# A recurrent two-layer kernel: GpSimd's order round two scan states, TensorE's order behind the transposes, two steps moved on VectorE

## The chip, the cores and the metric

One core of one Trainium2 chip. The metric is the device time of one execution in microseconds. The core's engines are TensorE (PE, with its weight loads as PEld), VectorE (DVE), ScalarE (ACT), GpSimd (POOL) and SyncE (SP), which here only issues DMAs. Each engine works through its own instructions strictly in the order in which the program issues them; between engines there are only semaphores.

## The reference, cut to what matters

```python
x = L0_attn_x                                  # (4, 1024, 128)
xn = _layernorm(x)
s = retention(xn)        # q, k, v, scores times a decay mask, summed over the past
g = silu(ternary_ffn(xn))# h = silu(x w1) * (x w2); gelu(h h1); gelu(h h2); w3
x = x + s * g            # layer zero
xn = _layernorm(x)
# layer one, left side (a state-space scan)
x_ssm, gate = split(xn @ W_in + b_in)
x_conv = silu(causal_conv4(x_ssm) + conv_b)
B, C = split(x_conv @ W_x + b_x)               # 16 states each
h = exp(-exp(A_log)) * h + x_conv[:, :, None] * B[:, None, :]   # over time
y = sum_n(C * h) + D * x_conv
s = (y * silu(gate)) @ W_out + b_out
# layer one, right side: the top half of the tokens by a router score go through an FFN
g = silu(xn + [token is in the top half] * sigmoid(score) * ffn(xn))
x = x + s * g
```

## The kernel before, in words

**Tiling.** The four sequences of 1024 tokens are cut into eight units of 512 tokens (`HALF`). A unit's features lie on the 128 partitions, its tokens along the free axis. The scan over time has 128 x 16 = 2048 rows, so each unit has 16 scan steps k = 0 to 15, one tile of 128 rows by 512 tokens each.

**Stages.** The program runs through periods p = -1 to 8 (`PERIODS`), each of 16 slots s (`slots`, those of p = -1 from slot 9). In period p the units have roles (`units`): n = p does layer one's front (its norm, convolution, gate, B, C, score), v = p + 1 does layer zero, w = p + 2 gets its layer-zero norm, t = p - 1 finishes its scan, ranking and token update, e = p - 2 is put out. Slots 0 to 7 hold the scan steps 8 to 15 of t, slots 8 to 15 the steps 0 to 7 of n (`scanned`). A function `slot(p, s)` in each engine's block lists what that engine does in a slot: the order is written out by hand, and an engine whose next instruction waits holds up all that stands behind it.

**One scan step.** SP spreads 8 rows of `xc` over 128 partitions by DMA (`spread_x` into `xs`, a ring of 5); DVE multiplies with B (`times_b` into `xbank`; `Bt` for k < 3, `bbank` after) and scans (`scan` into `hs`, a ring of 8); POOL multiplies with C (`weigh_states`); PE sums four steps at a time into `ybank` (`gather_y`, quads 0 to 3). `gate_y` (DVE) multiplies `ybank` by the gate into `yg`, which PE projects (`project_out`) for DVE's `output` and POOL's `add_output`.

**Hidden layers of layer zero.** Each 128x512 tile is made on PE (`hidden`), taken twice on ACT (`plain`, and rounded, `hidAh`/`hidBh`), and POOL subtracts the two (`low_hidden` into `hidAl`/`hidBl`); PE's next layer needs the difference of all four tiles. `plain` is a ring of three, so ACT's tile i waits for POOL's tile i - 3. z, h1 and h2 have four tiles each: h1 is made in slots 5 to 8, h2 in slots 10 to 13.

**Norms.** DVE takes the statistics (`stats_l0`, slot 7; `stats_l1`, slot 2), POOL makes the root (`rstd_l0`, slot 8, before that slot's scan state; `rstd_l1`, slot 2), ACT normalizes (`norm_l0`, slot 9, before `take_u`, which empties the bank that the first h2 tile needs; `norm_l1`, slot 2), PE transposes (`retention_in`, slot 9, before h2; `norm_to_features`, slot 3).

**Banks.** `bank0d` holds in turn z2(1), scores, z2(3), outer and s of layer zero: each waits until DVE has taken the one before (`L0_DVE`). `bank1a` holds xnT, conv, gate, B, C, score and its column in that order (`L1_ACT`), each after ACT has taken the one before.

**PE before, slots 3 to 9:** z1(3), z2(3), mod_down, norm_to_features | outer, gather_y quad 2, convolve | project_out, gate, h1(0) | B, h1(1), C | rank, h1(2), score | h1(3), score_column, quad 3 | rank, retention_out, retention_in.

## Time and profile before

| | |
|---|---|
| median of 3 runs | 537.83 us (537.45 to 539.37) |
| the profiled execution | 537.29 us, of which the span is 535.5 us |
| PE busy | 441.1 us, 82% of the span |
| DVE busy | 394.2 us, 74% |
| POOL busy | 387.8 us, 72% |
| ACT busy | 291.4 us, 54% |
| the chain that ended last | PE 34%, DVE 22%, issue 17%, POOL 16%, ACT 8%, DMA 2% |

All times of the trace are microseconds from the start of the span. The stretch from slot 14 of one period to slot 14 of the next shows in the trace as the distance between two quad-0 sums in `ybank`; six such distances, from 114.5 to 455, are the steady part, ahead of them is the filling, behind them (80 us) the last unit, in which layer zero has nothing left to do. The page's letters are the engines; "idle before" is what an engine waited ahead of an instruction, and the name behind the arrow is what ended the wait. No engine is busy all of the time, and the chain changes engine many times in a period; the rows below are from the period of n = 3 (its slots 0 to 15 lie between about 231 and 289) unless they say otherwise.

### The profile page before, as it was taken

The page shows a single profiled execution, that of the slowest core. Times are in us where ns is not written, and L with a number is a line of the kernel's source. Part 1 is how long each engine was busy: PE and PEld are TensorE (multiplying, and loading weights), DVE is VectorE, ACT ScalarE, POOL GpSimd, SP SyncE. Part 2 cuts the span into 40 slices and gives each one's busy share as a digit, 9 for nine tenths or more (in the row PEclk, how much of TensorE's full clock was granted, in tenths as well). Part 3 has the DMA queues.
Part 4 walks back from the last instruction along what each step waited for, and adds up shares of the span by engine and source line. Part 5 has one row for each costly group of instructions (what it writes and reads, how often), then busy time and mean ns, then how long its engine had stood idle before and what let it go on. Part 6 is the DMA issues. An engine that isn't in the chain of part 4 may idle for free.

```text
span 535.5 us, 6095 instructions
## 1 busy us (share of the span) xinstructions
PE 441.1 (82%) x1796; PEld 261.6 (49%) x1807; DVE 394.2 (74%) x683; ACT 291.4 (54%) x475; POOL 387.8 (72%) x317
## 2 busy tenths in 40 slices
PE   0794968898989898998889897989799889875843
PEld 0573645654555555654565455545555457321221
DVE  2282042959779895879688986798698949978985
ACT  3763654685467646763667556764676466333300
POOL 1672561788499859987699859984998679863682
PEclk9996979899999999999999999999999999898865
DMA  8300004421342215320633144312523053306330
GB/s 319 140 21 4 1 1 125 112 78 40 88 110 79 80 35 161 99 80 20 194 84 78 40 138 127 76 54 62 144 73 96 20 159 79 98 23 174 86 91 20
DMA packets 25379, 46.97 MB, mean 88 GB/s; under 512 B 3072, under 2 KB 4096, under 8 KB 25088
## 3 DMA queue, kind: packets, MB, share of 16 engines
q1 hardware_dynamic: 24336, 45.13, 29.9%
q10 hardware_dynamic: 1008, 1.41, 0.8%
q8 instruction: 18, 0.29, 0.2%
q14 instruction: 17, 0.14, 0.1%
HBM read 42.33 MB, written 4.19 MB: 87 GB/s over the span
## 4 chain that ended last, share of the span: by engine, by line
PE 34%; DVE 22%; issue 17%; POOL 16%; ACT 8%; DMA 2%; SPq 0%; DVEq 0%; POOLq 0%; ACTq 0%
PE bank0a L940 18%; DVE hs L1371 9%; DVE xbank L1348 6%; POOL hs L556 6%; PE bank0a L1059 5%; POOL hidAl L518 2%; ACT xn L692 2%; POOL hidBl L518 2%; PE ybank L1085 2%; PE bank1a L1020 2%; POOL g L530 2%; POOL xr L538 1%; POOL q L507 1%; DMA Bt<-w_in 1%; DVE st L1276 1%
## 5 line engine op out<-in xcount | busy, mean ns | idle before, releaser
L556 POOL TENSOR_TENSOR hs<-hs,Ct 128x512 f32<-128x512 f32 x127 | 170.9, 1350 | 34.5 <-DVE hs L1371 22.3
L518 POOL TENSOR_TENSOR hidAl<-plain,hidAh 128x512 fp32r<-128x512 f32 x48 | 63.7, 1327 | 39.3 <-ACT hidAh L651 33.2
L1371 DVE TENSOR_TENSOR_SCAN hs<-decay,carry,xbank 128x512 f32<-128x512 f32 x63 | 80.5, 1278 | 8.0 <-DVE xbank L1348 0.5
L518 POOL TENSOR_TENSOR hidBl<-plain,hidBh 128x512 fp32r<-128x512 f32 x48 | 67.0, 1396 | 26.4 <-ACT hidBh L651 18.5
L1371 DVE TENSOR_TENSOR_SCAN hs<-decay,xbank 128x512 f32<-128x512 f32 x64 | 78.0, 1219 | 5.6 <-DVE xbank L1348 0.5
L1348 DVE TENSOR_TENSOR xbank<-xs,bbank 128x512 f32<-128x512 f32 x104 | 71.5, 687 | 1.3
L650 ACT ACTIVATE plain<-bank0a,col 128x512 f32<-128x512 f32 x64 | 44.1, 689 | 44.7 <-PE bank0a L940 43.5
L940 PE MATMUL bank0a<-hidBh,hTh 128*128 128x512 f32 x128 | 57.8, 452 | 1.7 <-ACT q L683 1.7
L940 PE MATMUL bank0a<-hidAh,hTh 128*128 128x512 f32 x128 | 56.4, 441 | 1.7 <-ACT q L683 1.7
L940 PE MATMUL bank0a<-hidAl,hTh 128*128 128x512 f32 x128 | 51.7, 404 | 0.0
L940 PE MATMUL bank0a<-hidBl,hTh 128*128 128x512 f32 x128 | 50.7, 396 | 0.0
L1085 PE MATMUL ybank<-hs,gat 128*32 128x512 f32 x254 | 36.9, 648 | 16.2 <-POOL hs L556 16.1
L1348 DVE TENSOR_TENSOR xbank<-xs,Bt 128x512 f32<-128x512 f32 x24 | 26.7, 1114 | 27.6 <-ACT Bt L638 19.6
L1020 PE MATMUL bank1a<-ynT,w_conv 128*128 128x512 f32 (+3 forms) x64 | 34.3, 645 | 0.0
L1319 DVE SCALAR_TENSOR_TENSOR beats<-srow,scol,earlier 128x512 bf16<-128x512 f32 x32 | 34.3, 1071 | 0.0
L758 ACT ACTIVATE fh<-bank0a,col 128x512 f32<-128x512 f32 x32 | 21.3, 686 | 23.7 <-PE bank0a L1059 23.6
L1059 PE MATMUL bank0a<-ynT,lw 128*128 128x512 f32 x64 | 33.8, 635 | 0.0
L1271 DVE TENSOR_TENSOR sc<-bank0d,sc 128x512 f32<-128x512 f32 x8 | 5.5, 691 | 36.0 <-ACT sc L670 36.0
L940 PEld LDWEIGHTS bank0a<-hidBh,hTh 128*128 128x128 f32 x128 | 24.3, 190 | 11.4 <-issue 3.1
L940 PEld LDWEIGHTS bank0a<-hidAh,hTh 128*128 128x128 f32 x128 | 24.7, 193 | 10.2 <-ACT q L683 2.5
L1068 PE MATMUL bank1d<-fh,w2l 128*128 128x512 f32 x56 | 29.3, 608 | 0.0
L638 ACT ACTIVATE xc<-bank1a,b_conv 128x512 f32<-128x512 f32 x8 | 5.5, 687 | 43.1 <-PE bank1a L1020 43.1
(190 smaller groups left out, 938.8 us busy)
## 6 DMA issues: line engine op xcount, KB each, us to landing
xs<-x_rows SPq DMA_DIRECT2D x128, 256.0 KB, 3.5
xt<-x_tok SPq DMA_DIRECT2D x8, 256.0 KB, 4.8
xr<-x_feat SPq DMA_DIRECT2D x8, 256.0 KB, 7.6
x_rows<-xc SPq DMA_DIRECT2D x8, 256.0 KB, 2.3
out<-xr SPq DMA_DIRECT2D x7, 256.0 KB, 2.3
fh<-h_w SPq DMA_DIRECT2D x1, 1024.0 KB, 9.6
hs<-h_w SPq DMA_DIRECT2D x1, 1024.0 KB, 11.4
lw<-l_w ACTq DMA_DIRECT2D x1, 640.0 KB, 5.3
```

The source lines that it names most:

```text
L518: pool.tensor_tensor(low[:, m, :], plain[:, k % NPLAIN, :], high[:, m, :].bitcast(F32), ALU.subtract).then_inc(hidden_low, 1)
L556: pool.tensor_tensor(h, h, Ct[:, hs_(u)], ALU.mult).then_inc(p_ready, 1)
L650: act.activation(plain[:, k % NPLAIN, :], bank[:], ACT.Gelu, scale=scale(kind + "_s", m))
L758: act.activation(fh[:, m, :], bank[:], ACT.Gelu_apprx_tanh, bias=scale("b1", m)).then_inc(l0_act_done, 1)
L940: last = pe.matmul(bank[:], w, x, start=(start and n == 0), stop=(stop and n == len(passes) - 1))
L1020: last = pe.matmul(bank1a[:, s:HALF], w_conv[:, k, :], ynT[:, t % NYNT, 0:HALF - s], start=(s == 0), stop=(k == 0))
L1059: pe.matmul(bank[:], W_1[:, ck(m)], ynT[:, t % NYNT, :], start=True, stop=True).then_inc(l0_act_full, 1)
L1068: last = pe.matmul((bank0d if t == UNITS - 1 else bank1d)[:], w2l[:, kt, :], fh[:, kt, :], start=(kt == 0), stop=(kt == KT - 1))
L1085: pe.matmul(ybank[rows, :], gat[:, at:at + P // QUAD], hs[:, step(u, QUAD * quad + j) % NSTATES, :], start=False, stop=(quad == NGRP // QU ...
L1319: dve.scalar_tensor_tensor(bt, row, s_i, earlier[:, at:at + HALF], ALU.subtract, ALU.is_lt).then_inc(beats_ready, 1)
L1348: dve.tensor_tensor(xbank[:], xs[:, i % NROWS, :], b, ALU.mult).then_inc(xb_ready, 1)
L1371: dve.tensor_tensor_scan(hs[:, i % NSTATES, :], decay[:, gr:gr + 1].broadcast_to([P, HALF]), xbank[:], 0.0 if u % 2 == 0 else carry[:, k:k ...
```

## The change

**GpSimd.** Before, slots 6 to 9 each began with one `low_hidden("h1")`, then (slot 8) `rstd_l0`, then the scan state. Now slots 6 and 7 begin with the scan states k = 14 and 15; behind 15 follow `rstd_l0(w)` and h1(0); h1(1) and h1(2) come ahead of the states k = 0 and 1 (slots 8 and 9), h1(3) behind the state k = 1. `weigh_update` goes from slot 6 to slot 10. **TensorE.** Behind the transposes of slot 3 comes the convolution, then project_out and B, and only then outer, quad 2 and the gate; **ScalarE** takes B before the gate. **VectorE.** `stats_l1` stands behind z_product(1) in slot 1 instead of behind `times_b` of slot 2; `mask_scores` before z_product(2) instead of behind it; `memory` in slot 6 instead of 4; `gate_y` in slot 11 instead of 9. In the prologue POOL does one h1 tile fewer before `rstd_l0(1)`.

```diff
-        L1_ACT += [(_k, _n) for _k in ("xnT", "conv", "gate", "B", "C", "score", "score_col")]
+        L1_ACT += [(_k, _n) for _k in ("xnT", "conv", "B", "gate", "C", "score", "score_col")]
...
                 if v is not None:
                     if 1 <= s < 1 + KT:
                         low_hidden("z", v, s - 1)
-                    elif 6 <= s < 6 + KT:
-                        low_hidden("h1", v, s - 6)
+                    elif s in (8, 9):
+                        low_hidden("h1", v, s - 7)
...
-                if w is not None and s == 8:
-                    rstd_l0(w)
                 if u is not None:
                     weigh_states(u, k)
+                if w is not None and s == 7:
+                    rstd_l0(w)
+                if v is not None and s in (7, 9):
+                    low_hidden("h1", v, 0 if s == 7 else 3)
...
-                if t is not None and s == (1 if t == UNITS - 1 else 6):
+                if t is not None and s == (1 if t == UNITS - 1 else 10):
                     weigh_update(t)
...
-            for m in range(KT - 1):
+            for m in range(KT - 2):
                 low_hidden("h1", 0, m)
...
                     if s == 5:
                         convolved(n)
+                        take_B(n)
                         take_gate(n)
...
-                    if s == 6:
-                        take_B(n)
-                    elif s == 7:
+                    if s == 7:
                         take_C(n)
...
-                        elif s == 4:
-                            outer(v)
...
-                    if s in (1, 4) and t is not None:
-                        gather_y(t, 1 if s == 1 else 2)
+                    if n is not None and s == 4:
+                        convolve(n, (3, 2, 1, 0))
                     if s == 5 and e is not None and e != UNITS - 2:
                         project_out(e)
-                    if n is not None:
-                        if s == 4:
-                            convolve(n, (3, 2, 1, 0))
-                        elif s == 5:
-                            project("gate", n, W_IN[:, P:2 * P])
-                        elif s == 6:
-                            project_x("B", n, W_B)
+                    if n is not None and s == 5:
+                        project_x("B", n, W_B)
+                    if v is not None and s == 5:
+                        outer(v)
+                    if s in (1, 5) and t is not None:
+                        gather_y(t, 1 if s == 1 else 2)
+                    if n is not None and s == 5:
+                        project("gate", n, W_IN[:, P:2 * P])
...
-                    elif s == 2:
-                        stats_l1(n)
...
+                if v is not None and s == 2:
+                    mask_scores(v)
                 if v is not None and s < KT:
                     z_product(v, s)
+                if n is not None and s == 1:
+                    stats_l1(n)
                 if v is not None:
-                    if s == 2:
-                        mask_scores(v)
-                    elif s == 4:
+                    if s == 6:
                         memory(v)
...
-                    elif t < UNITS - 1 and s == 9:
+                    elif t < UNITS - 1 and s == 11:
                         gate_y(t)
```

## Rows read from the trace of the kernel before

**Rows 1.** Stretches by period: length; busy time of PE, PEld, DVE, ACT, POOL; clock; DMA.

```profile
114.50:171.10 56.60, 50.99 (x223) 30.49 (x225) 44.38 (x83) 34.23 (x58) 44.38 (x37) 1.00 0.30 79
228.00:285.90 57.90, 51.85 (x224) 30.88 (x230) 47.21 (x88) 35.05 (x59) 47.43 (x39) 1.00 0.34 92
...
400.60:455.00 54.40, 50.52 (x221) 30.47 (x226) 43.95 (x66) 31.81 (x52) 45.07 (x35) 1.00 0.33 88
455.00:535.00 80.00, 51.23 (x165) 18.92 (x166) 65.66 (x98) 20.28 (x31) 47.95 (x39) 0.79 0.31 82
```

**Rows 2.** Timeline of POOL, n = 3: start, duration, line, tiles, idle before.

```profile
259.85 1.27 POOL L518 TENSOR_TENSOR hidBl<-plain,hidBh 128x512 fp32r<-128x512 f32 x1 [5.15 <-ACT hidBh L651]
...
266.98 1.27 POOL L556 TENSOR_TENSOR hs<-hs,Ct 128x512 f32<-128x512 f32 x1
...
269.43 1.02 POOL L485 TENSOR_TENSOR rstd<-ve,half_neg 128x4 f32<-128x4 f32 x1
```

**Rows 3.** Timeline of PE, n = 3: z2(3), outer, project_out, C, quad 3, h2(0).

```profile
244.09 0.48 PE L940 MATMUL bank0d<-xnTh,w12h 128*128 128x512 f32 x1 [1.79 <-DVE sc L1240]
...
246.88 1.13 PE L913 MATMUL bank0d<-xn,xt 128*128 128x128 f32 x8 [0.79 <-DVE plain L1264]
...
253.13 1.02 PE L1108 MATMUL bank1d<-Bt,lw 128*128 128x512 f32 x2
...
260.40 1.12 PE L1030 MATMUL bank1a<-xc,lw 128*128 128x512 f32 x2 [0.55 <-ACT Bt L638]
...
268.30 1.06 PE L1085 MATMUL ybank<-hs,gat 128*32 128x512 f32 x8 [1.31 <-POOL hs L556]
...
273.83 0.50 PE L940 MATMUL bank0a<-hidBh,hTh 128*128 128x512 f32 x1 [0.58 <-ACT q L683]
```

**Rows 4.** Timeline of ACT, n = 3: ynT, xc, Bt, bbank (keep_B), norm_l0.

```profile
246.13 0.60 ACT L638 ACTIVATE ynT<-bank1a 128x512 f32<-128x512 f32 x1 [0.68 <-PE bank1a L999]
...
253.39 0.69 ACT L638 ACTIVATE xc<-bank1a,b_conv 128x512 f32<-128x512 f32 x1 [5.42 <-PE bank1a L1020]
...
259.66 0.69 ACT L638 ACTIVATE Bt<-bank1a,col 128x512 f32<-128x512 f32 x1
...
267.85 0.61 ACT L748 ACTIVATE bbank<-Bt 128x512 f32<-128x512 f32 x1
270.89 1.65 ACT L692 ACTIVATE xn<-xt,ve,rstd 128x128 f32<-128x128 f32 x4 [2.42 <-POOL ve L488]
```

**Rows 5.** Timeline of DVE, n = 3: stats_l1, scan, mask, times_b(0), gate_y, token_weights.

```profile
239.76 0.86 DVE L1276 BATCH_NORM_STATS2 st<-yn 128x6 f32<-128x128 f32 x4
...
241.28 1.21 DVE L1371 TENSOR_TENSOR_SCAN hs<-decay,xbank 128x512 f32<-128x512 f32 x1
...
243.26 0.68 DVE L1240 TENSOR_TENSOR sc<-bank0d,mask 128x512 f32<-128x512 f32 x1
...
260.92 0.76 DVE L1348 TENSOR_TENSOR xbank<-xs,Bt 128x512 f32<-128x512 f32 x1 [2.40 <-ACT Bt L638]
...
269.51 0.69 DVE L1380 TENSOR_TENSOR Bt<-ybank,gate 128x512 f32<-128x512 f32 x1 [3.46 <-PE ybank L1085]
...
279.54 0.67 DVE L1334 SCALAR_TENSOR_TENSOR g<-bank1d,g 128x512 f32<-128x512 f32 x1
```

**Rows 6.** Instructions of line 556: duration min/median/max.

```profile
L556 POOL TENSOR_TENSOR hs<-hs,Ct x127: 1262/1278/1815, 98.4 to 525.0; 128x512 f32<-128x512 f32 x127
```

**Rows 7.** Timeline of PE in period 0: retention_in.

```profile
100.30 0.65 PE L892 MATMUL bank0a<-ident,xn 128*128 128x128 f32 x4 [1.30 <-ACT xn L692]
```

**Rows 8.** Timeline of PE in period 6: quad 3.

```profile
439.84 1.06 PE L1085 MATMUL ybank<-hs,gat 128*32 128x512 f32 x8 [1.26 <-POOL hs L556]
```

**Rows 9.** Timeline of ACT in period 7: ynT.

```profile
470.83 0.60 ACT L638 ACTIVATE ynT<-bank1a 128x512 f32<-128x512 f32 x1 [0.81 <-PE bank1a L999]
```

**Rows 10.** Timeline of PE in period 7: quad 2.

```profile
471.88 1.06 PE L1085 MATMUL ybank<-hs,gat 128*32 128x512 f32 x8 [1.08 <-POOL hs L556]
```

**Rows 11.** Timeline of DVE in period 7: times_b(0).

```profile
483.66 0.70 DVE L1348 TENSOR_TENSOR xbank<-xs,Bt 128x512 f32<-128x512 f32 x1 [2.66 <-DMA xs<-x_rows]
```

## The prediction

> **What bounds the kernel now.** I read the page's busy shares first, then the table of stretches, the list of waits, the chain, and last the timelines of one period, engine by engine. The stretches show that PE is busy 50.99 us of 56.60 in the first steady one and 51.85 of 57.90 in that of n = 3, at full clock, while DVE and POOL have some 10 us of slack each [rows 1]. So a steady period is PE's own work plus about 6 us in which PE waits, and five such stretches and a sixth without w make up the time from 114.5 to 455 (rows 1 show the first, the third and the sixth) [rows 1]. The reader is to see in PE's timeline where these 6 us lie: 1.79 before z2(3), 0.79 before outer, 0.55 before C, 1.31 before quad 3, 0.58 before h2(0) [rows 3], which makes 5.0; the rest lies before the transposes ahead of it. Each has another engine behind it. z2(3) waits for the mask on DVE, whose stream is gapless there [rows 5]. C waits for ACT, which has to empty `bank1a` of B and does that only behind h1(0), at 259.66 [rows 4]. Quad 3 waits for POOL's state 15 at 266.98, and that is the important one: POOL sits idle 5.15 us until 259.85 for the first h1 tile, with state 14, add_output, weigh_update, state 15 and the root of the norm all queued behind it [rows 2]. The root (269.43) is what ACT's norm_l0 waits for 2.42 us [rows 2, 4], and h2(0) on PE follows norm_l0 through the transposes and take_u, 273.83 - 270.89 = 2.94 us after its start [rows 3, 4].
>
> **The change in one steady period, from PE's start of slot 0.** (a) Mask first takes its 0.68 us from z2(3)'s wait [rows 5]. Against that, `stats_l1` starts earlier by about 0.6 us, but times_b of slot 2, which ran ahead of it, now stands behind it: it was 0.69 long and the scan behind it came directly at 241.28 [rows 5]. Net the scan is 0.2 to 0.3 later. z2(3) starts 0.4 earlier. The statistics' earlier end is worth at most 0.1, since POOL is busy with a z tile until it takes the root, 0.1 behind DVE. Running sum -0.4.
> (b) The transposes come 0.4 earlier. The 0.79 us before outer goes, but the convolution now stands directly behind ynT, which ACT takes 0.60 us long right behind the transposes [rows 4]: a wait of 0.7 to 0.8 in its place. Net 0.
> (c) Convolution, then project_out, 1.02 us [rows 3], which covers ACT's xc, 0.69 us and some 0.2 of handover [rows 4]; B then finds xc ready. Its matmuls (as large as project_out's) only move from behind h1(0) to ahead of it. Outer (1.13 as its first matmul group stands in the row [rows 3]) and quad 2 only move too, and they give ACT the time to empty B before the gate. Quad 2's states are finished long before; the ring of eight `hs` tiles needs it for the states 0 to 3 of n, 5 us later still. `memory` in slot 6 finds outer done, and retention_out wants it only in slot 9; load_tok, on SP in slot 6 behind the spreads, waits for outer in slot 5 and delays nothing. At the end of h1(1) the sum is still -0.4.
> (d) C no longer waits for ACT: 0.7 us counted from h1(1)'s last start to 260.40 (0.55 as listed [rows 3]). Sum -1.1, at the end of h1(3).
> (e) POOL. Its 5.15 us idle stretch [rows 2] takes in state 14, add_output, state 15 and the root; DVE has scan 15 by about 257 and the statistics of w by 258.8, so the root is done by about 260.2, and h1(0) goes at 260.2 instead of 259.85, a delay of 0.4 that ACT doesn't feel: it wants that place in `plain` only for h1(3), 5 us on. So quad 3 finds state 15 seven microseconds old: -1.3, sum -2.5.
> (f) norm_l0 no longer waits for POOL. It now stands behind keep_B, which ran from 267.85 for 0.61 [rows 4] and moves by (d): 267.85 + 0.61 - 1.1 = 267.35 instead of 270.89 [rows 4], -3.5. PE gets to the transposes at about 269.0, as ACT is done with them. h2(0) follows 2.94 later: 270.3 instead of 273.83. **Sum -3.5**; in even n, where the mask comes in a slightly tighter stream, I get -3.3. I take 3.35.
> (g) Can the rest follow? DVE: times_b(0) loses its 2.40 and gate_y its 3.46 us of waiting [rows 5]; with Bt taken at about 253 and the spread rows landed by 257 the first is limited by DVE alone. DVE comes to token_weights at about 275 instead of 279.54 [rows 5], in odd n ahead of PE's shift; in even n it waits there for PE's ranks and moves with it, as before. gate_y in slot 11 is done at 271.5, PE's quad 0 wants it at 282. weigh_update in slot 10 is done at about 271, token_weights wants it at 275. POOL's h1(3) ends at about 268, h2 wants it at 271.8. From low_xn on POOL has the same order as before, shifted with PE, and its last h2 tile had 1.5 us in hand before w3. So the whole 3.35 stays.
>
> **The other periods.** p = 1 to 5: 5 x 3.35 = 16.8. p = 0 has no scan states before slot 8, so POOL is not late; what is left is C's 0.7 and part of the 1.30 us before the transposes [rows 7], less B's xc, which no project_out covers: 1.0. p = 6 has no w: (a) to (e) with quad 3's 1.26 [rows 8], 2.4. p = 7 has neither v nor w and is set by DVE and a DMA: ynT is taken by 471.43 [rows 9], the convolution started only behind quad 2, which waited 1.08 for state 11 and began at 471.88 [rows 10]. Now it starts with ynT, and the statistics come 0.5 sooner: 1.9 us earlier, and xc, its store, the spread and times_b(0), which waited 2.66 us for that DMA [rows 11], follow; from there to the end DVE has hardly a gap and the same work. In the prologue POOL does rstd_l0(1) one tile sooner but waits there for DVE either way; the held-back tile has 5 us before h2. Nothing.
> Sum: 16.8 + 1.0 + 2.4 + 1.9 = 22.1. The profiled execution took 537.29 us, of which 535.5 span; it is 0.54 under the median of 537.83. 537.3 - 22.1 = 515.2, against the median 515.7. I say **515.4**.
>
> **What the sum doesn't show.** The extra price of two engines working side by side where POOL was idle. A POOL multiplication takes 1.26 us alone and 1.82 at worst beside DVE, median 1.28 [rows 6]. Four instructions move into the gap: between 0 and 2.2 us, of which 5 us of slack to quad 3 swallow all. Hence 0, with the worst case among the rivals.
> The Trainium skill speaks against filling that gap: its page "SBUF — State Buffer", section "Who interferes with whom", has VectorE's two-SBUF-input tensor_tensor and GpSimd's reads share a port pair that one holds and the other waits for. By it every moved state could cost itself up to one DVE instruction; the trace agrees that the same POOL form has two lengths, and the sum by that rule would be that of the rival R1 at most.
>
> **Rivals.**
> R1, POOL becomes the bound behind the gap. From h1(3) on ACT (266.7) to the last h2 tile, POOL has 12 instructions, now with weigh_update's place right ahead of h2. At 1.28 they take 15.4 us, at 1.75 21, so they end between 282 and 287.7; PE's w3 wants the last at 286.7. At worst 1.0 us of the gain is lost in each of five periods, and if low h1(3) comes late too, 1 more: 515.4 + 5 to 10 = 520 to 525. For: POOL is 47.43 us busy of 57.90 [rows 1], and of the new 54.4 that is 87%. Against: its median is 1.28 [rows 6].
> R2, more than I count: the waits I left (0.7 ahead of the convolution, 1.3 before z2(3), 0.6 before h2) shrink, or the last stretch gains from keep_B and the gate coming sooner: up to 1 us in six periods, 509. Against: each is one engine's latency.
> R3, nothing: the POOL wait was idle time that another chain (scan on DVE from slot 0 to 5, then PE) would have had anyway, and only C's and the mask's 1.1 us stay, given back in the next period's residual wait: 537. Against it speaks that quad 3 and h2(0) themselves stand waiting on PE [rows 3].
> R4, slower. POOL's head now waits for scan 15 and the statistics of w before it does any h1 tile. Were DVE late there, h1(3) on ACT would wait for a free `plain` and all of PE's h2 behind it. It decides from 4 us of DVE's delay against the replay, costs 1 us per us beyond that, and with 8 us late PE loses 4 - 3.35 net: 5 x 0.65 more than before, 540.5. For: DVE is gapless from slot 0 to 8. Against: it gets no new work, only 0.3 us from (a).
>
> **How the numbers follow.** Forecast (511 to 519.5) 0.66; R1 0.18; R2 0.08; R3 0.04; R4 0.04. The range for 8 in 10 takes in the forecast, most of R1 and a part of R2: 510 to 522.5. A measurement of this kernel can tell about 0.5% (2.7 us) from no change: faster 0.92, same 0.04, slower 0.04.
>
> **What would show it.** Steady stretches of 53.3 (even) to 54.4 (odd) us with PE busy unchanged; no POOL wait ahead of the states 14 and 15, and only a small one ahead of h1(0); no wait before C and quad 3; ACT's norm_l0 directly behind keep_B; a wait of 0.7 before the convolution; 1.3 before z2(3); times_b(0) and gate_y on DVE without waits; period 7's times_b(0) still waiting for its DMA. Wrong would be: h2 or w3 on PE waiting for POOL (R1), or ACT's h1(3) waiting for POOL (R4).

## The result and the profile after

The changed kernel takes **523.79 us** (median of 4 runs, 519.55 to 525.08) against 537.85 us (537.45 to 539.37) for the kernel before on the same chip: a ratio of 0.972, 95% interval 0.966 to 0.978. It is faster, as forecast, but by 14 us and not by 22, and the range (510.0 to 522.5) missed it by 1.3. Its profiled execution took 522.57 us, of which 520.8 span.

The same stretches of the changed kernel as [rows 1] (length; busy time of PE, PEld, DVE, ACT, POOL; granted clock; DMA share), cut at the same point of the period, with period 5 added as the third line:

```profile
115.40:170.05 54.65, 50.51 (x225) 30.49 (x228) 45.76 (x83) 34.20 (x58) 44.45 (x36) 1.00 0.31 78
224.00:278.70 54.70, 51.37 (x226) 30.87 (x227) 49.40 (x89) 34.99 (x59) 47.70 (x39) 1.00 0.36 100
332.60:388.70 56.10, 52.77 (x226) 31.49 (x227) 49.56 (x89) 34.86 (x59) 47.60 (x39) 0.97 0.31 88
388.70:441.30 52.60, 50.24 (x222) 30.56 (x226) 46.80 (x67) 31.99 (x52) 44.82 (x36) 1.00 0.32 92
441.30:520.00 78.70, 49.63 (x167) 18.76 (x166) 65.09 (x96) 20.14 (x31) 47.00 (x38) 0.83 0.28 83
```

PE has the same work in a shorter stretch: 3.3 us of waiting are left of 54.70 in the period of n = 3, where 6.05 were left of 57.90. DVE is busy 2.2 us longer there for the same tiles (49.40 against 47.21 in rows 1), POOL 0.3.

TensorE in the period of n = 3 (start, duration, line, tiles, idle before), to be laid beside [rows 3]; the lines are z2(3), the convolution, project_out, outer, quad 3 and h2(0):

```profile
240.17 0.47 PE L941 MATMUL bank0d<-xnTh,w12h 128*128 128x512 f32 x1 [1.91 <-DVE sc L1240]
242.95 1.10 PE L1021 MATMUL bank1a<-ynT,w_conv 128*128 128x512 f32 x2 [0.78 <-ACT ynT L640]
...
247.12 1.02 PE L1109 MATMUL bank1d<-Bt,lw 128*128 128x512 f32 x2
...
249.15 1.05 PE L914 MATMUL bank0d<-xn,xt 128*128 128x128 f32 x8
...
262.23 1.06 PE L1086 MATMUL ybank<-hs,gat 128*32 128x512 f32 x8
...
266.62 0.50 PE L941 MATMUL bank0a<-hidBh,hTh 128*128 128x512 f32 x1 [0.57 <-ACT q L685]
```

The waits before outer, C and quad 3 are gone; the convolution waits 0.78 for ynT; the wait before z2(3) has grown from 1.79 to 1.91 instead of falling to 1.3. POOL and ACT in the same stretch, beside [rows 2] and [rows 4]: POOL's states 14 and 15 with add_output's product between them, the root, h1(0) and h1(1); ACT's keep_B and norm_l0.

```profile
250.26 1.28 POOL L556 TENSOR_TENSOR hs<-hs,Ct 128x512 f32<-128x512 f32 x1
251.50 1.28 POOL L538 TENSOR_TENSOR xr<-g,xr 128x512 f32<-128x512 f32 x1
253.89 1.30 POOL L556 TENSOR_TENSOR hs<-hs,Ct 128x512 f32<-128x512 f32 x1 [1.12 <-DVE carry L1375]
255.29 1.46 POOL L485 TENSOR_TENSOR rstd<-ve,half_neg 128x4 f32<-128x4 f32 x1
256.83 0.20 POOL L488 TENSOR_TENSOR ve<-negmean,rstd 128x4 f32<-128x4 f32 x1
256.99 2.97 POOL L518 TENSOR_TENSOR hidBl<-plain,hidBh 128x512 fp32r<-128x512 f32 x2
```

```profile
263.17 0.61 ACT L750 ACTIVATE bbank<-Bt 128x512 f32<-128x512 f32 x1
263.69 1.64 ACT L694 ACTIVATE xn<-xt,ve,rstd 128x128 f32<-128x128 f32 x4
```

POOL's idle 5.15 us [rows 2] now hold both states and the root; ACT's norm_l0 stands directly behind keep_B. Quad 3's state is ready 7.0 us before PE wants it. This part of the forecast came true line by line.

The distances between the quad-0 sums (for n = 0 at 113.52 before and 114.39 after, then from one n to the next):

| | to n = 0 | p = 1 | 2 | 3 | 4 | 5 | 6 | 7 | from there to the end |
|---|---|---|---|---|---|---|---|---|---|
| before | 113.52 | 56.60 | 56.85 | 57.88 | 56.85 | 57.88 | 54.42 | 43.84 | 37.66 |
| changed | 114.39 | 54.65 | 53.89 | 54.71 | 53.89 | 56.14 | 52.61 | 41.59 | 38.93 |
| difference | +0.9 | -1.95 | -2.96 | -3.17 | -2.96 | -1.74 | -1.8 | -2.25 | +1.3 |
| forecast | -1.0 | -3.35 | -3.35 | -3.35 | -3.35 | -3.35 | -2.4 | -1.9 for both | |

The differences add up to -14.7 us where the forecast had -22.1. The seven us that are missing lie in four places: the filling (1.9), period 1 (1.4), period 5 (1.6), and the rest in small amounts in the other steady periods and in the end (2.5). Each row is one execution. In a second profile of the changed kernel (span 524.4 us) periods 1 to 6 have the same lengths to 0.15 us, but quad 0 of n = 0 starts at 115.71 and period 7 takes 43.30: what is said below of the filling and of period 7 holds for the profiled execution only. The experiments go after these places and after what each part of the change was worth.

### The profile page after: what moved, and what is told of

It is laid out like the page before. It is cut to its first block, busy times and chain, and to the rows that moved or that the text cites. A ratio compares the mean times of both kernels' runs of the same rounds, so it can differ in the third digit from the quotient of the medians.

```text
span 520.8 us, 6106 instructions
## 1 busy us (share of the span) xinstructions
PE 438.9 (84%) x1807; PEld 262.1 (50%) x1807; DVE 401.0 (77%) x683; ACT 291.4 (56%) x475; POOL 388.5 (75%) x317
## 4 chain that ended last, share of the span: by engine, by line
PE 59%; DVE 15%; ACT 10%; issue 9%; POOL 3%; DMA 3%; SPq 0%; DVEq 0%; ACTq 0%; POOLq 0%
PE bank0a L941 27%; PE bank1a L1021 6%; DVE hs L1371 5%; PE bank0a L1060 5%; DVE xbank L1348 4%; PE ybank L1086 3%; PE bank1a L1031 3%; PE bank1a L1006 3%; ACT xn L694 2%; DVE plain L1264 2%; DMA Bt<-w_in 2%; PE bank0d L914 1%; DVE st L1276 1%; PE ybank L1081 1%; PE bank0d L930 1%
## 5 line engine op out<-in xcount | busy, mean ns | idle before, releaser
L556 POOL TENSOR_TENSOR hs<-hs,Ct 128x512 f32<-128x512 f32 x127 | 164.2, 1295 | 44.0 <-DVE hs L1371 25.4
L518 POOL TENSOR_TENSOR hidAl<-plain,hidAh 128x512 fp32r<-128x512 f32 x48 | 67.3, 1407 | 16.9 <-ACT hidAh L653 10.7
L941 PE MATMUL bank0a<-hidBh,hTh 128*128 128x512 f32 x128 | 56.0, 438 | 1.7 <-ACT q L685 1.7
L941 PE MATMUL bank0a<-hidAh,hTh 128*128 128x512 f32 x128 | 55.3, 432 | 1.7 <-ACT q L685 1.7
L1086 PE MATMUL ybank<-hs,gat 128*32 128x512 f32 x254 | 35.8, 630 | 9.0 <-POOL hs L556 9.0
L1348 DVE TENSOR_TENSOR xbank<-xs,Bt 128x512 f32<-128x512 f32 x24 | 29.5, 1227 | 4.3 <-DMA xs<-x_rows 3.4
L941 PEld LDWEIGHTS bank0a<-hidAl,hTh 128*128 128x128 f32 x128 | 24.7, 193 | 6.8 <-issue 1.4
```

The costliest lines, as they stand in the source:

```text
L518: pool.tensor_tensor(low[:, m, :], plain[:, k % NPLAIN, :], high[:, m, :].bitcast(F32), ALU.subtract).then_inc(hidden_low, 1)
L556: pool.tensor_tensor(h, h, Ct[:, hs_(u)], ALU.mult).then_inc(p_ready, 1)
L941: last = pe.matmul(bank[:], w, x, start=(start and n == 0), stop=(stop and n == len(passes) - 1))
L1086: pe.matmul(ybank[rows, :], gat[:, at:at + P // QUAD], hs[:, step(u, QUAD * quad + j) % NSTATES, :], start=False, stop=(quad == NGRP // QU ...
L1348: dve.tensor_tensor(xbank[:], xs[:, i % NROWS, :], b, ALU.mult).then_inc(xb_ready, 1)
```

## Experiments

In the text all differences are taken between medians; the kernel before had medians of 537.76 to 538.69 beside these runs, so a difference of 1 us between two of them says little.

| | what is different | median us | range | ratio to before, 95% |
|---|---|---|---|---|
| changed | (measured again) | 523.79 | 520.13 to 526.16 | 0.970 (0.9675 to 0.9734) |
| 1 | changed, statistics back | 520.29 | 516.05 to 521.35 | 0.965 (0.9625 to 0.9672) |
| 2 | changed, statistics and mask back | 521.65 | 519.79 to 521.87 | 0.969 (0.9658 to 0.9711) |
| 3 | changed, two DVE instructions to ACT | 518.16 | 514.58 to 518.82 | 0.961 (0.959 to 0.9639) |
| 4 | changed, z1(3) repeated from period 0 | 514.63 | 513.81 to 516.41 | 0.955 (0.9521 to 0.9569) |
| 5 | changed, z1(3) repeated from period 1 | 519.02 | 517.97 to 520.61 | 0.964 (0.9605 to 0.966) |
| 6 | before, z1(3) repeated from period 0 | 535.27 | 532.77 to 536.62 | 0.995 (0.993 to 0.9965) |
| 7 | before with the new POOL order | 529.05 | 526.55 to 530.44 | 0.982 (0.9784 to 0.9864) |
| 8 | changed with the old POOL order | 548.27 | 547.36 to 551.35 | 1.020 (1.0154 to 1.0236) |
| 9 | before with the new DVE order | 549.48 | 546.5 to 550.01 | 1.020 (1.0168 to 1.0228) |
| 10 | as 8, B behind h1(0) | 542.69 | 536.82 to 544.9 | 1.007 (1.0032 to 1.0099) |
| 11 | 3 and a shorter 4 together | 511.51 | 508.57 to 515.21 | 0.950 (0.9459 to 0.9542) |

### The statistics of layer one (1)

```diff
+                    elif s == 2:
+                        stats_l1(n)
...
-                if n is not None and s == 1:
-                    stats_l1(n)
```

> Only stats_l1 goes back to slot 2, behind times_b; the mask stays first and all else is as changed. Theory port: in the changed kernel the short addition of eps in stats_l1 (line 1285) took 0.80 us instead of 0.21 because it now runs while GpSimd works on a z tile, so the early statistics gain nothing and the scan behind them, the mask and z2(3) come 0.8 us later than they could. Then line 1285 is back at about 0.2 us, z2(3) waits about 1.2 instead of 1.9 us, the steady periods are 0.6 to 0.8 us shorter (54.0 odd, 53.2 even), and the time is 4 us below the changed kernel's. Rival, what stands before z2(3) is no path: period and time as in the changed kernel (54.7 and 53.9, within 1 us).

The reason to try it is DVE's timeline of the changed kernel in slot 1: the last z product, the statistics (the second-last of them line 1285, an addition on 128x4 elements), times_b, scan, mask. Beside it stands POOL's z tile.

```profile
236.13 0.28 DVE L1281 BATCH_NORM_AGGREGATE mv<-st 128x2 f32<-128x6 f32 x3
236.45 0.80 DVE L1285 TENSOR_SCALAR ve<-mv 128x4 f32<-128x4 f32 x1
237.16 0.16 DVE L1286 TENSOR_SCALAR negmean<-mv 128x4 f32<-128x4 f32 x1
237.23 0.69 DVE L1348 TENSOR_TENSOR xbank<-xs,bbank 128x512 f32<-128x512 f32 x1
238.02 1.22 DVE L1371 TENSOR_TENSOR_SCAN hs<-decay,xbank 128x512 f32<-128x512 f32 x1
...
239.35 0.68 DVE L1240 TENSOR_TENSOR sc<-bank0d,mask 128x512 f32<-128x512 f32 x1
```

```profile
235.96 1.27 POOL L518 TENSOR_TENSOR hidAl<-plain,hidAh 128x512 fp32r<-128x512 f32 x1
```

Line 1285 ends at 237.25, POOL's tile at 237.23. The groups of that line, of the changed kernel and then of this one (count, busy us, mean ns, idle us before):

```profile
L1285 DVE TENSOR_SCALAR ve<-mv 128x4 f32<-128x4 f32 x8 | 5.8, 730 | 0.3
```

```profile
L1285 DVE TENSOR_SCALAR ve<-mv 128x4 f32<-128x4 f32 x8 | 2.3, 284 | 0.3
```

The means hide two lengths: in periods 1 to 6 the addition takes 209 to 221 ns in its old place and 802 to 817 in the new one; the two at the ends of the program take the same in both. So the early place put the addition beside a POOL tile, and it took 0.6 us longer; the tile of slot 1 stayed the thing that POOL had to finish before the root, so the statistics' earlier end bought nothing. With them back the steady periods are 53.1 and 53.9 instead of 53.9 and 54.7, z2(3) waits 1.1:

```profile
236.71 0.47 PE L941 MATMUL bank0d<-xnTh,w12h 128*128 128x512 f32 x1 [1.12 <-DVE sc L1240]
```

and the median is 3.5 us lower, near the theory's 4. The step of the statistics in the change costs 0.8 us a period, of which the longer addition is 0.6. The Trainium skill, "SBUF — State Buffer", section "Who interferes with whom", says that tensor_scalar can enter a mode in which it takes the port pair it has in common with GpSimd, and whoever holds that pair blocks the other for the whole instruction; the end of the 0.80 us together with POOL's agrees with that. That the instruction was in that mode no run here shows.

### Mask and statistics together (2)

```diff
-                if v is not None and s == 2:
-                    mask_scores(v)
                 if v is not None and s < KT:
                     z_product(v, s)
+                if v is not None and s == 2:
+                    mask_scores(v)
```

and the statistics back as in the run before.

> The changed kernel with both VectorE steps of slots 1 and 2 back where they were: the statistics of layer one behind times_b of slot 2, the mask behind z_product(2). Against the run with the statistics alone back (520.29, z2(3) waits 1.2 in its steady periods) this tells what the mask is worth. Theory, VectorE's part is worth nothing taken together, because the mask's gain is eaten by the statistics' port: 523 to 525 like the changed kernel, z2(3) waiting 1.6 to 1.9, and 0.4 to 0.5 more per period than with the statistics alone back. Rival, the mask's place is worth nothing and all of the statistics' loss is saved: 520 to 521, z2(3) waiting 1.2.

The steady periods are 54.6 and 53.7, against 53.9 and 53.1 with the mask first and 54.7 and 53.9 in the changed kernel; z2(3) waits 1.80 in the period of n = 3. So the mask's place is worth 0.65 us a period, the statistics' costs 0.8, together a little less than nothing. By the medians the kernel lies between, at 521.65: 1.4 above the run with the statistics alone back, and 2.1 below the changed kernel, which shows one fall of the clock more in its profile (below). Both expectations missed the time, 523 to 525 and 520 to 521. The wait of 1.80 is the theory's (1.6 to 1.9), and the mask is worth more than its 0.4 to 0.5 a period.

### The same statistics with two instructions on ACT (3)

```diff
             def norm_l1(t):
+                act.activation(ve1[:, cc], mv1[:, cc, 1], ACT.Copy, bias=EPS).then_inc(eps1, 1)
+                act.activation(negmean1[:, cc], mv1[:, cc, 0], ACT.Copy, scale=-1.0).then_inc(negmean1_ready, 1)
```

and lines 1285 and 1286 taken from DVE; the statistics stay in slot 1.

> stats_l1 stays early, but its two short instructions (addition of eps, sign of the mean) run on ScalarE, right ahead of norm_l1. Theory port: VectorE loses the 0.96 us of these two rows altogether, the scan, the mask and z2(3) come 0.8 to 0.9 us sooner, GpSimd's root starts where it did (it is held by a z tile), periods 0.6 to 0.8 us shorter than in the changed kernel, time 4 us lower. Rival, the delay of the scan comes from the order (times_b behind the statistics) and not from the long row: the periods shorten by the 0.3 us of the two short rows at most, 1.5 us in all.

518.16, 5.6 below the changed kernel and 2.1 below the run with the statistics back. The addition takes 202 ns on ACT, z2(3) waits 1.01, the periods are 53.0 and 53.7 to 54.1. These are the periods of run 1 to within 0.15 us, so the 2.1 us between the two medians are not in them. What is left of the wait was not followed.

### The clock, and the filling (4, 5, 6)

The granted clock of the changed kernel in four stretches of 2 us of period 5 (length; busy times; clock last but two):

```profile
346.00:348.00 2.00, 0.86 (x3) 0.19 (x1) 1.86 (x4) 0.74 (x2) 1.15 (x2) 1.00 0.17 10
348.00:350.00 2.00, 1.23 (x3) 0.90 (x4) 1.90 (x5) 1.59 (x5) 1.28 (x1) 0.78 0.41 121
350.00:352.00 2.00, 2.00 (x6) 0.89 (x4) 1.97 (x4) 0.52 (x1) 1.79 (x2) 0.50 0.00 0
352.00:354.00 2.00, 1.22 (x5) 0.56 (x4) 1.90 (x3) 1.70 (x3) 1.31 (x2) 0.86 0.00 0
```

Behind the wait before z2(3) (PE busy 0.86 of 2 us) the clock falls to half, 1.2 instead of 2.4 GHz, from 349.1 to 352.6. What runs at that level is mod_down and the transposes; the convolution finds the full clock again. PE in that stretch:

```profile
349.45 1.91 PE L1069 MATMUL bank1d<-fh,w2l 128*128 128x512 f32 x2
351.15 1.06 PE L1000 MATMUL bank1a<-ident,yn 128*128 128x128 f32 x4
352.99 1.10 PE L1021 MATMUL bank1a<-ynT,w_conv 128*128 128x512 f32 x2 [0.78 <-ACT ynT L640]
```

In the period of n = 3 these take 1.02, 0.60 and 1.10 us. Period 5 is 56.14 us long, its sister of n = 3 54.71. The repeat of the changed kernel shows the same in the same place (56.29; 350.3 to 353.7), the kernel before none in any steady period. Periods 1 and 3 of the changed kernel have the same waits and no fall. To take the wait away without taking work out, z1(3)'s matmuls are done four times, all with the same result:

```diff
+                    if m == KT - 1 and not first:
+                        for _ in range(3):
+                            split_product(bank, [(w12h[:, 0, ck(m)], w12l[:, 0, ck(m)], xnTh[:], xnTl[:])])
                     split_product(bank, [(w12h[:, 0, ck(m)], w12l[:, 0, ck(m)], xnTh[:], xnTl[:])]).then_inc(l0_act_full, 1)
```

> TensorE repeats the two matmuls of z1(3) three times before the counted ones, in each period from 0 on: 1.4 us more of work in the place where it waits 1.9 us for the mask; the result is the same. Theory clock: the runs of the changed kernel differ (519.6 to 525.1 us) because behind the wait of 1.9 us and the one of 0.8 us shortly after it the granted clock falls to 0.5 for some 4 us in some periods, at 1.4 us each. Then here the granted clock between 110 and 440 us is 1.00 throughout, the wait before z2(3) is about 0.5 us, the steady periods are 54.7 and 53.9 as before, and the median is 520 to 521 with a spread under 1.5 us. Rival, the falls have nothing to do with that wait: spread and median as in the changed kernel, 523 to 524.

514.63, 9.2 below the changed kernel and more than any theory had. The five steady periods are 54.65, 53.89, 54.72, 53.88 and 54.71: the same lengths as the undisturbed ones of the changed kernel. So the copies hide in the wait (0.54 are left of it), and the clock accounts for 1.4 us in each period in which it falls. But the profile has the larger part elsewhere: quad 0 of n = 0 starts at 110.17 instead of 114.39. To separate the two, the copies were left out of period 0 (`if m == KT - 1 and t >= 2`):

> The repeated z1(3) matmuls only from period 1 on, none in period 0. The filled kernel of before was 9 us under the changed one, of which by its trace 2.5 us lie ahead of 48 us (a wait of TensorE without a releaser that was gone) and 1.8 us in period 0, where the clock is back sooner. Theory clock: the falls in the steady periods make up the rest, 4 to 5 us; here the time is 516 to 519, the mean clock 0.955 to 0.965. Rival, it was the head of the program and period 0 alone: 521 to 524 and a mean clock of 0.95.

519.02, at the upper end of the theory, with the steady periods again 54.7 and 53.9, period 5 at full clock throughout:

```profile
331.10:385.80 54.70, 52.65 (x227) 32.01 (x229) 49.40 (x89) 35.01 (x58) 47.70 (x39) 1.00 0.35 92
```

It is 4.8 below the changed kernel and 4.4 above run 4. Of these 4.4 the copies in period 0 can have only a part: of the 4.2 between the two profiles 1.8 lie ahead of quad 0 of n = 0, and 2.4 lie in period 7, where no copies run; there the store of `xc` took 4.38 us to land in this execution and 2.00 in the changed kernel's. Last the kernel before with the copies in all periods but the first:

> The kernel before with the two matmuls of z1(3) done four times instead of once in every period but the first, as in the run at 514.63 of the changed kernel (which was 9.2 less). The copies (6 x 0.4 us) lie in the wait ahead of z2(3), 1.79 us here. Theory, the copies' gain there was 7 falls and the head of the program; before shows few falls in its steady periods, only the head's and period 0's effect (2.5 + 1.8) is to be had: 533 to 537. Rival, the filling helps before as much as the changed kernel: 529 to 531. Rival, its copies only cost: 538 to 541.

535.27, 2.5 below the kernel before, within the theory's 533 to 537; the periods are the old ones to 0.03 us (56.57, 56.83, 57.85, 56.85, 57.85), and quad 0 of n = 0 starts at 111.11 instead of 113.52. What goes there is a wait of PE in period 0 that the profile puts to no other engine. First the kernel before, then the same with the copies:

```profile
46.22 0.77 PE L922 MATMUL bank0a<-sc,xn 128*128 128x128 f32 x2 [4.93 <-issue]
49.12 0.59 PE L923 MATMUL bank0a<-q,mem 128*128 128x128 f32 x2 [2.13 <-issue]
```

```profile
47.28 0.77 PE L922 MATMUL bank0a<-sc,xn 128*128 128x128 f32 x2 [5.31 <-issue]
47.84 0.63 PE L923 MATMUL bank0a<-q,mem 128*128 128x128 f32 x2
```

The wait of 2.1 to 2.4 us is gone in all four kernels with copies and there in all nine without. The clock is down round it too, for 10.2 to 10.3 us in each of the nine and 6.8 to 6.9 in each of the four (44.0 to 54.3 before, 44.9 to 51.8 in run 6). Both hold in run 5, whose copies run first in period 1, long after this instruction. So it is not their running that ends it but something in the longer program (the wait is put to issue, to no other engine); what, is open. What the copies do in period 0 by running shows in the clock: it is down from 76.1 to 82.9 in the changed kernel and from 73.5 to 80.3 in run 5, 6.8 us in both, and from 75.3 to 78.8 in run 4, which has copies there.

So three things were taken away at once, and only one belongs to this change: falls in steady periods (1.4 to 1.6 us each, none in the kernel before, where the copies changed nothing from n = 0 on), the wait at 50 (2.1 us, in either kernel), and half of a long fall in period 0. The 4.8 us between run 5 and the changed kernel are one of medians; their two profiles are 2.0 apart: quad 0 of n = 0 comes 2.4 sooner, period 5 is 1.4 shorter and period 7 is 2.1 longer, with the late store. The rest of the 4.8 stays open.

### POOL's order alone (7)

The kernel before with the new block of POOL, including weigh_update's slot; TensorE, ScalarE and VectorE as they were.

> The kernel before with GpSimd's block of the changed one alone. By the prediction's steps (e) and (f) quad 3 loses its wait of 1.3 us and norm_l0 stands directly behind keep_B, 267.85 + 0.61 = 268.5 instead of 270.9: -2.4 us in each of periods 2 to 5, 1.2 in period 1 (no add_output in front), 1.3 in period 6: 12 us, 526. Rival, the B order is needed for it, since h1(0) and the rest come as late as before: under 6 us.

529.05, 9.6 below the kernel before as measured beside it (538.69), between the theory's 12 and the rival's 6. Periods 1 to 6 are 55.29, 54.70, 55.35, 54.65, 55.35 and 53.43: -1.3, then -2.15, -2.5, -2.2, -2.5 and -1.0. These six make the 12; in the profile 1.2 are lost again in the filling and 1.6 in period 7, which no experiment followed. The waits before quad 3 are gone, those before outer and C are there:

```profile
241.83 0.47 PE L942 MATMUL bank0d<-xnTh,w12h 128*128 128x512 f32 x1 [1.80 <-DVE sc L1242]
244.62 1.13 PE L915 MATMUL bank0d<-xn,xt 128*128 128x128 f32 x8 [0.79 <-DVE plain L1266]
258.14 1.13 PE L1032 MATMUL bank1a<-xc,lw 128*128 128x512 f32 x2 [0.55 <-ACT Bt L640]
269.05 0.50 PE L942 MATMUL bank0a<-hidBh,hTh 128*128 128x512 f32 x1 [0.57 <-ACT q L685]
```

This is steps (e) and (f) by themselves, which the forecast put at 3.5 - 1.1 = 2.4. And from here to run 2 (TensorE and ScalarE's new order too, and gate_y and memory in their new slots) the periods fall by another 0.7 to 1.0, where step (d) had 0.7.

### Everything but POOL's order (8, 9, 10)

> The changed kernel with GpSimd's block of the kernel before. Quad 3 and norm_l0 hang on GpSimd's chain from the first h1 tile, which comes 0.2 us later than before; the wait before C goes, but quad 3 then waits that much longer. Steady periods 56.6 to 58, only period 7 gains its 1.9 us: 534 to 538. Rival, the parts add up: all but GpSimd is worth 14 - 12 = 2 us and more, 532 or less.

548.27: 9.6 slower than before where all theories had it at or below. The parts do not add up: POOL's order alone takes 10 us off, the others alone put 10 on, together they take 14 off. The lines that show it are POOL's h1(0) and PE's quad 3:

```profile
265.06 1.29 POOL L518 TENSOR_TENSOR hidBl<-plain,hidBh 128x512 fp32r<-128x512 f32 x1 [6.54 <-ACT hidBh L651]
```

```profile
273.46 1.59 PE L1084 MATMUL ybank<-hs,gat 128*32 128x512 f32 x8 [2.94 <-POOL hs L556]
```

From the start of the last transposes to POOL's h1(0) it was 259.85 - 245.49 = 14.36 us before, here 265.06 - 249.79 = 15.27: 0.9 more, with B now ahead of h1(0). With POOL's old order h1(0) is the head of the chain h1(0), state 14, add_output, state 15, quad 3, so what stands ahead of it on PE is paid. Two runs take it apart. The clock has a share too: in run 8 it fell in each of periods 2 to 6, each time beside the wait of 2.7 to 2.9 before quad 3. The first is the kernel before with DVE's new block alone:

> The kernel before with VectorE's whole block of the changed one (mask first, statistics in slot 1, memory in slot 6, gate_y in slot 11) and nothing else. Theory, VectorE's part alone is worth nothing: 537 to 540. Rival one, the forecast's step (a) (-0.4 in seven periods): 534.5 to 536. Rival two, this part is what made everything but GpSimd's order slower than before: 544 to 549.

549.48: as slow, without B having moved, and half a us above rival two's range. The periods that have no fall of the clock are 1.1 to 1.2 longer than before. PE in period 5 (z2(3), outer, C, quad 3):

```profile
366.35 0.47 PE L940 MATMUL bank0d<-xnTh,w12h 128*128 128x512 f32 x1 [1.92 <-DVE sc L1240]
369.80 1.13 PE L913 MATMUL bank0d<-xn,xt 128*128 128x128 f32 x8 [1.45 <-DVE plain L1264]
383.32 1.13 PE L1030 MATMUL bank1a<-xc,lw 128*128 128x512 f32 x2 [0.54 <-ACT Bt L638]
391.65 1.07 PE L1085 MATMUL ybank<-hs,gat 128*32 128x512 f32 x8 [1.74 <-POOL hs L556]
```

With the mask ahead of z_product(2), and the statistics' 0.8 ahead of both, z_product(3) ends 0.8 later, and outer, which in the old order of PE comes directly behind, waits 1.45 instead of 0.79 [rows 3]; memory in slot 6 puts its 1.24 us, and 1.1 of waiting for project_out, ahead of state 15, and quad 3 waits 1.74 instead of 1.31. Periods 1 and 3, with a fall of the clock each, are 2.7 and 1.5 longer than before. In the changed kernel outer stands behind the convolution and two projections, and neither it nor quad 3 waits. What the whole of VectorE's part costs there no run shows: run 2 takes back only two of its four steps.

The second is run 8 with B behind h1(0) again on PE and ACT:

> The changed kernel with GpSimd's order of before, as in the run at 548.27, but B again behind h1(0) on TensorE and ScalarE; convolution and project_out stay directly behind the transposes. Theory, that run was slow because B (0.9 us) delays h1(0), and with GpSimd's old order the first h1 tile heads the chain to states 14 and 15, quad 3 and the norm's root: 0.9 less in each of six periods, POOL waiting 5.2 to 5.8 for h1(0) instead of 6.54, 540 to 544. Rival, B is not it (VectorE's part or the convolution's place is): 546 to 549.

542.69, 5.6 below run 8 and in the theory's range. Its undisturbed periods are 57.2 and 58.0, 0.2 to 0.4 above before. From the transposes to h1(0) it is 14.1 us in period 5 and was 15.3 in run 8's period of n = 3, so B's place delays h1(0) by 1.2; POOL waits 5.37 for it in period 5, within the expected 5.2 to 5.8, and 8.29 in the period of n = 3, where the clock fell in the transposes and the convolution. Quad 3 waits 1.73 to 1.75. How much of the 5.6 is B's is not shown to the tenth: the profile of run 8 has five periods with a fall, this one two. B ahead of h1(0) and DVE's delays each cost time where POOL's chain begins with h1(0).

### Statistics on ACT and copies together (11)

Run 3 with z1(3) three times instead of four.

> The two short instructions of stats_l1 on ScalarE and z1(3)'s two matmuls repeated twice (0.9 us of the 1.0 us that it still waits for the mask). If the two losses are separate they add: 518.2 less what the fill took from the changed kernel (9.2) less 1 because the wait was shorter already: 509 to 511, mean clock 0.965, spread under 2 us. Rival, with the wait at 1.0 us there were no falls left to prevent and the fill is worth only the head and period 0: 513 to 515.

511.51, 12.3 below the changed kernel and 0.950 of before: the best of the runs, and 0.5 above the expected 509 to 511. Its periods are those of run 3 (53.74, 53.06, 54.06, 53.07, 53.79), which had no falls there either; quad 0 of n = 0 starts at 110.82 instead of run 3's 112.81.

### The end, read from the traces

From times_b(0) of the last unit to the end of the span it is 535.5 - 483.66 = 51.84 us before, 526.5 - 474.69 = 51.81 in run 7, and 520.8 - 467.70 = 53.10 in the changed kernel, 547.9 - 494.81 = 53.09 in run 9. So it is not POOL's order but DVE's, and by the lines below gate_y's slot. DVE before, from scan 1 of the last unit:

```profile
486.71 1.28 DVE L1371 TENSOR_TENSOR_SCAN hs<-decay,carry,xbank 128x512 f32<-128x512 f32 x1
487.91 0.67 DVE L1380 TENSOR_TENSOR Bt<-ybank,gate 128x512 f32<-128x512 f32 x1
488.49 1.40 DVE L1348 TENSOR_TENSOR xbank<-xs,Bt 128x512 f32<-128x512 f32 x1
```

and in the changed kernel:

```profile
470.76 1.28 DVE L1371 TENSOR_TENSOR_SCAN hs<-decay,carry,xbank 128x512 f32<-128x512 f32 x1
472.15 1.79 DVE L1348 TENSOR_TENSOR xbank<-xs,Bt 128x512 f32<-128x512 f32 x1
...
479.94 0.67 DVE L1380 TENSOR_TENSOR Bt<-ybank,gate 128x512 f32<-128x512 f32 x1
480.52 1.39 DVE L1319 SCALAR_TENSOR_TENSOR beats<-srow,scol,earlier 128x512 bf16<-128x512 f32 x1
```

times_b(2) ends 3.18 us behind scan 1's start in both: in slot 9 gate_y ran in time that times_b(2) would otherwise spend beside POOL's state (1.79 instead of 1.40, the first of them without gate_y). In slot 11 its 0.6 us are added, and the comparison behind it takes 1.39 where the one before took 0.72: 1.25 in all. That gate_y alone does it was not run by itself.

## Why the prediction was right and wrong

**Right: POOL, quad 3, norm_l0.** Steps (d), (e), (f) and (g) hold. Quad 3, C and outer wait no more; norm_l0 stands directly behind keep_B; from z2(3) to h2(0) it is 26.45 us now and was 29.74, -3.3. Run 7 gave 2.2 to 2.5 a period for (e) and (f), forecast 2.4. h2 and w3 on PE wait for no POOL tile, so the rival R1 is out although the time is in its range of 520 to 525; its condition (POOL's multiplication longer) went the other way, the mean to 1295 from 1350 ns. That the time fell into R1's range is chance. R4's condition didn't come in either: POOL waits 1.12 for scan 15 and then nothing for h1(0).

**Wrong: step (a), -0.4 before z2(3).** It came as +0.1 (17.24 us from quad 0 to z2(3) in the period of n = 3, 17.12 before). The mask gave 0.65 (runs 1 and 2) of its 0.68. The term that failed is the statistics' +0.2 to 0.3, which run 1 measured as 0.8: the forecast moved some 1.5 us of small instructions and gave them their old durations, and one of them took 0.80 instead of 0.21 beside POOL's z tile. The forecast weighed the shared ports for POOL's moved states, where they cost nothing that counts, and not for DVE's moved instructions, one of which grew by 0.6. In periods 2 to 4 this is 0.5 each, of which (d) to (f) gave about 0.2 back by being a little better than forecast: 1.0 in the three together.

**Wrong: period 1, -3.35.** It was read from the period of n = 3. In period 1 there is nothing to be put out, so neither project_out nor add_output: before, POOL's chain was one multiplication shorter, quad 3 did not wait and the period had 56.60, not 57.88. The changed kernel has 54.65, hardly less than its 54.71 with them, because B, with no project_out ahead of it, waits 0.87 for xc. That wait is not new: before, the gate waited 0.78 for xc in this period, so here there was one wait less to take away.

PE in the changed kernel:

```profile
139.62 1.10 PE L1031 MATMUL bank1a<-xc,lw 128*128 128x512 f32 x2 [0.87 <-ACT xc L640]
```

So 1.3 of the 3.35 were never there, and the 56.60 stood in the rows beside the 57.90 [rows 1].

**Wrong: period 0, -1.0.** C's 0.7 went, but B waits 0.95 for xc where the gate waited 0.86 for it, and the convolution 0.73 for ynT where outer waited 0.86; what z2(3) waits less (1.17 instead of 1.83) the transposes wait more (1.71 instead of 1.04); the 1.30 us before the transposes of layer zero [rows 7] stayed at 1.30 (at 101.17). From the outer of the filling, which starts at 29.44 and did at 28.35, to quad 0 of n = 0 it is 84.95 us and was 85.17: 0.2 gained of the 1.0, and the program's first 30 us were 1.1 longer in this execution. Why is open; that part varies: quad 0 of n = 0 starts between 112.8 and 115.8 in the kernels without copies.

**Not in the sum: the clock.** Period 5 lost 1.43 of its gain to a fall to 1.2 GHz (the third line of the first block), behind the wait of 1.91 before z2(3). The prediction had no term for it. Step (b)'s exchange of waits, 0.79 before outer for 0.78 before the convolution, came as forecast, and the fall is over before the convolution starts. Why the clock falls in that period and not in 1 and 3 is open, and so is whether the change makes falls more frequent. For it: there are none in the steady periods of the kernel before, one each in two profiles of the changed kernel, and two or more in runs 8, 9 and 10. Against TensorE's new order as the reason: run 9 has the old one, and run 2, with the new one and waits of 1.80 and 0.78, has no fall in five steady periods.

**Half right: periods 6 and 7.** Period 6 gave 1.8 of 2.4 and is short by step (a) too. The start of the last unit came sooner: times_b(0) at 467.70 is 27.42 behind quad 0 of n = 6, and was 29.66: -2.2 where the forecast said -1.9. In the second profile of the changed kernel it is 29.54, only 0.1 less than before: there the clock fell from 459.5 to 462.9, in period 7's convolution. So this gain is there only when that fall is not. Behind it the forecast took "the same work"; gate_y's slot and a comparison that now falls beside POOL give 1.25 back. What the forecast missed is that gate_y cost nothing in its old place, where times_b(2) ends at the same distance with it and without.

The sum is 1.9 + 1.4 + 1.6 + 0.6 + 0.9 for periods 0, 1, 5, 6 and the last stretch, and 1.0 for periods 2 to 4, 7.4 together.

## What to carry to other kernels

A step's gain read from one steady period holds only for periods with the same members; read the first, the second and the last for themselves before multiplying. When instructions are moved on VectorE, look at what GpSimd runs beside their new place: a 128x4 addition of 0.21 us took 0.81 there and the step cost 0.8 us a period, and two small instructions given to ScalarE brought that back. And parts of a change that each move a different engine's order are not worth what they are worth alone: here VectorE's part alone cost 12 us with GpSimd's old order, GpSimd's part alone gave 10, and all parts together gave 14.

## What the runs showed of the hardware

- An addition on VectorE of 128x4 elements, both sides in SBUF, takes 209 to 221 ns in one place of the steady periods and 802 to 817 ns in another, where it ends together with GpSimd's running tensor_tensor (237.25 and 237.23); the same on ScalarE takes 202 ns on average (run 3).
- TensorE's granted clock fell to half (1.2 GHz) for 3.4 us behind a wait of 1.91 us in one steady period, and not in two others with the same wait; the fall lengthened the period by 1.4 to 1.6 us. With 1.4 us of that wait filled with matmuls there was none in the five steady periods of either kernel profiled.
- A wait of TensorE of 2.1 to 2.4 us that is put to no engine (issue) was gone in each of the four kernels whose program was longer by some matmuls, even where these ran only later, and the low clock round it lasted 6.8 us there instead of 10.2; in the kernel before the copies took 2.5 us off in all (535.27 against 537.76). The cause isn't known.
